# Row 8 of the mirrored matrix dealt into the second sweep, and the third sweep ends with row 7

## The reference, cut to what matters

```
x = layernorm(x + L0(x, adj))      # L0: h = adj @ (adj.T @ e), normalized, + x
T1 = adj @ x                       # L1: a Chebyshev recurrence with K = 4
T2 = 2 * (adj @ T1) - x
T3 = 2 * (adj @ T2) - T1
out = x @ w[0] + T1 @ w[1] + T2 @ w[2] + T3 @ w[3] + bias
x = layernorm(x + out)
```

## Time and profile before

| | |
|---|---|
| median of 3 runs | 1171.82 us (1171.09 to 1174.2) |
| the profiled execution | 1168.52 us, its span 1166.7 us |
| PE busy, share of the span | 1082.1 us, 93% |
| DVE busy | 910.0 us, 78% |
| ACT busy | 330.9 us, 28% |
| DMA | 340.33 MB, 292 GB/s on average |
| mean granted clock of PE | 0.992 |

### The profile page before, as it was taken

The page is one execution under the profiler, slowest core; times in us unless marked ns, Lnnn a source line. Parts: engine busy times, 40 slices in busy tenths (PEclk is TensorE's granted clock), DMA queues, the critical chain, the costliest instruction groups (busy, mean ns, idle before and its releaser), DMA issues.

```text
span 1166.7 us, 13999 instructions
## 1 busy us (share of the span) xinstructions
PE 1082.1 (93%) x5050; PEld 467.6 (40%) x5050; DVE 910.0 (78%) x942; ACT 330.9 (28%) x592; POOL 265.8 (23%) x428
## 2 busy tenths in 40 slices
PE   6898999999999999868889999999899999988897
PEld 5454444444544544412333333443334444422332
DVE  2797788999989989898777767655577877678885
ACT  1555546645655654501111111000110000001111
POOL 0475735644534533610000000000000000001110
PEclk9999999999999999999999999999999999989999
DMA  9999999999999996999999999999599999999991
GB/s 284 273 292 288 285 278 319 301 297 292 270 287 296 273 284 174 224 298 346 278 347 345 327 322 322 296 288 261 163 319 347 337 335 348 338 282 346 343 333 30
DMA packets 366970, 340.33 MB, mean 292 GB/s; under 512 B 17500, under 2 KB 365700, under 8 KB 366932
## 3 DMA queue, kind: packets, MB, share of 16 engines
q1 hardware_dynamic: 257972, 232.24, 70.7%
q10 hardware_dynamic: 106496, 105.00, 31.0%
q0 software_dynamic: 2464, 2.59, 0.9%
HBM read 338.48 MB, written 1.31 MB: 291 GB/s over the span
## 4 chain that ended last, share of the span: by engine, by line
PE 55%; DVE 13%; SPq 12%; ACT 10%; issue 5%; ACTq 1%; POOL 1%; DMA 1%; DVEq 0%; POOLq 0%
PE bank L1267 26%; ACT terms L842 9%; SPq L378 7%; DVE turned L557 6%; PE bank L1335 5%; SPq L367 5%; PE bank L1280 5%; PE bank L1095 2%; PE bank L1135 2%; PE bank L1123 2%; PE bank L1107 2%; DVE shared L577 2%; PE bank L1147 2%; ACTq L321 1%; PE bank L1313 1%
## 5 line engine op out<-in xcount | busy, mean ns | idle before, releaser
L433 POOL COPY raw<-raw 32x512 f32<-32x512 f32 x320 | 195.3, 610 | 241.5 <-DVE raw L594 201.6
L1267 PE MATMUL bank<-turned,terms 128*128 128x512 f32 x528 | 235.5, 597 | 3.2 <-DVE turned L557 2.7
L577 DVE STREAM_TRANSPOSE shared<-shared 32x512 f32<-32x512 f32 x320 | 224.0, 700 | 4.1
L1095 PE MATMUL bank<-shared 128*64 128x256 f32 x1600 | 207.0, 387 | 10.3 <-DMA shared<-in_adj 10.3
L557 DVE STREAM_TRANSPOSE turned<-shared 128x2048 f32<-128x2048 f32 x70 | 160.2, 2301 | 62.4 <-PE bank L1267 34.2
L557 DVE STREAM_TRANSPOSE turned<-raw 128x2048 f32<-128x2048 f32 x70 | 159.7, 2296 | 52.7 <-PE bank L1267 37.4
L842 ACT COPY terms<-terms 32x512 f32<-32x512 f32 x312 | 192.2, 616 | 5.0 <-DVE terms L587 0.9
L326 POOL DMA_DIRECT2D out<-scratch x32 | 17.4, 551 | 597.2 <-DVE scratch L789 597.0
L1267 PEld LDWEIGHTS bank<-turned,terms 128*128 128x128 f32 x528 | 97.9, 190 | 131.1 <-issue 129.1
L1095 PEld LDWEIGHTS bank<-shared 128*64 128x64 f32 x1600 | 112.8, 137 | 92.0 <-issue 33.7
L1335 PE MATMUL bank<-turned,terms 128*64 128x512 f32 x360 | 97.0, 603 | 21.9 <-DVE turned L557 21.9
(11 more groups left out here) (158 smaller groups left out, 1085.7 us busy)
## 6 DMA issues: line engine op xcount, KB each, us to landing
shared<-in_adj SPq DMA_DIRECT2D x100, 1024.0 KB, 10.6
raw<-in_adj SPq DMA_DIRECT2D x100, 512.0 KB, 10.8
raw<-in_adj ACTq DMA_DIRECT2D x100, 512.0 KB, 12.9
shared<-in_adj SPq DMA_DIRECT2D x100, 512.0 KB, 10.5
shared<-in_adj ACTq DMA_DIRECT2D x100, 512.0 KB, 12.3
raw<-in_adj SPq DMA_DIRECT2D x80, 256.0 KB, 7.6
shared<-in_x SPq DMA_DIRECT2D x5, 256.0 KB, 4.7
xq<-in_x POOLq DMA_DIRECT2D x40, 32.0 KB, 6.0
```

The source lines that it names most:

```text
L433: last = nc.gpsimd.tensor_copy(moved[Q32 * c:Q32 * (c + 1), :, :, Q32 * q:Q32 * (q + 1)], beside[Q32 * q:Q32 * (q + 1), :, c, :, :])
L577: last = nc.vector.transpose(low_turned[Q32 * c:Q32 * (c + 1), :, :, Q32 * q:Q32 * (q + 1)], low[Q32 * q:Q32 * (q + 1), :, :, Q32 * c:Q32 ...
L1095: last = nc.tensor.matmul(t_bank[H * odd:H * (odd + 1), 0:PW], e[:, s * SB + b, :], panels[slot][:, s * SB + b, :], start=(k == 0 and b < ...
L1267: last = nc.tensor.matmul(sum_bank[parity][:, :], terms[:, c * GB + i, columns], turned[place][:, i * BANK:(i + 1) * BANK], start=(first a ...
```

## The change

It moves six tiles of T3's row 8, (8,7) to (8,2), from the third sweep into the second, in three pairs behind the three pairs of row 9; DIAG (8,8) and the place of (9,9), (9,8) stay. The second sweep is then n = 0 to 62 and the third n = 63 to 99. The order of what is left in the third sweep is another too: row 7's eight tiles, which stood at its start, stand at its end. Rows 8 and 9 are now open at the same time as two rows of T2, so row 8 is summed in bank 2 and one of the two output banks moves from bank 2 to bank 5. No instruction is added or removed but for waits: the same 100 tiles, 50 loads and 10 output rows are worked in another order.

```diff
-        out_bank = banks[1:3]
+        out_bank = [banks[1], banks[5]]
...
-        ROWS3 = [0, 7, 9, 8, 1, 6, 2, 5, 4, 3]
+        ROWS3 = [0, 9, 6, 8, 1, 5, 2, 4, 3, 7]
...
-        LAST_LOW = [(7, 3), None, (7, 2), (7, 1), (7, 0), (9, 0), (8, 3), (8, 2), (8, 1), (8, 0), (1, 0),
...
+        LAST_LOW = [(6, 2), None, (6, 1), (9, 0), (6, 0), (8, 0), (5, 2), (1, 0), (5, 1), (5, 0), (2, 0), (4, 1), (4, 0),
+                    (3, 1), (3, 0), (7, 3), (7, 2), (7, 1), (7, 0)]
...
                     late += [(DIAG, open_diag, open_diag), (LOW, NG - 1, open_diag + 1), (LOW, NG - 1, open_diag)]
+                    if open_diag < NG - 2:
+                        late += [(LOW, NG - 2, open_diag + 1), (LOW, NG - 2, open_diag)]
                     open_diag = None
```

More of the change, by code:

```diff
@@ L242, in resnorm_chebyshev @@
         ROWS2_ORDER = DOWN[1:]
-        ROWS3 = [0, 7, 9, 8, 1, 6, 2, 5, 4, 3]
-        LOW_BANK = {0: 6, 7: 7, 9: 0, 8: 6, 1: 7, 6: 6, 2: 7, 5: 6, 4: 7, 3: 6}
+        ROWS3 = [0, 9, 6, 8, 1, 5, 2, 4, 3, 7]
+        LOW_BANK = {6: 7, 0: 6, 9: 0, 8: 2, 5: 7, 1: 6, 2: 6, 4: 7, 3: 6, 7: 7}
         UP, DIAG, LOW = range(3)
-        LAST_LOW = [(7, 3), None, (7, 2), (7, 1), (7, 0), (9, 0), (8, 3), (8, 2), (8, 1), (8, 0), (1, 0),
-                    (6, 2), (6, 1), (6, 0), (2, 0), (5, 2), (5, 1), (5, 0), (4, 1), (4, 0), (3, 1), (3, 0)]
+        LAST_LOW = [(6, 2), None, (6, 1), (9, 0), (6, 0), (8, 0), (5, 2), (1, 0), (5, 1), (5, 0), (2, 0), (4, 1), (4, 0),
+                    (3, 1), (3, 0), (7, 3), (7, 2), (7, 1), (7, 0)]
         late = []
```

## The result

| | before | changed |
|---|---|---|
| median of 4 runs each | 1173.01 us (1171.09 to 1174.29) | 1162.9 us (1159.79 to 1163.79) |
| ratio | | 0.991, 95% interval 0.9885 to 0.9935 |
| profiled execution, its span | 1168.52, 1166.7 us | 1163.79, 1162.0 us |

The changed kernel is faster by 0.65 to 1.15%, some 10 us. The two profiled executions differ by 4.7 us only. That is no contradiction, but half of what has to be explained: the profile of before is of a short execution, 4.5 us under its median, and that of the changed kernel lies 0.9 us above its own.

The account below looks back on a forecast made before the run. It took PE and the DMA as near full in the second sweep, DVE with its waits in the third. 14.5 - 1.2 - 17.4 - 4.7 = -8.8 us, taken to the median 1171.82: 1163.0, range 1153 to 1170.

Parts of the forecast that it names:

- Term 1: Second sweep: six more LOW tiles and their loads make it longer, +14.5 us, bounds +10.3 and +18.1.
- Term 2: Change-over from the last UP tile to the first transposition behind row 0's finish: -1.2 us, bounds 0 and -4.5.
- Term 3: DVE's stretch after the change-over: 89.1 us against 106.5, with 6.7 of root waits, -17.4 us, bounds -24.1 and -11.2.
- Rival A: Change-over and third sweep: clock stays up (another -3.3 us), root waits vanish (-2.3 or -6.7), 1153 to 1158; chance 0.20.
- Term 4: The end behind DVE's last transposition: 12.8 us against 17.5, -4.7 us, bounds -4 and -5.
- B: Rows 0, 9, 6, 8 and 1: all three waits whole, change-over as before, gain only -1.4 us, 1170; chance 0.12.
- C: Third sweep: load issues hold ACT ahead of take_p at three rows, +8.9 us, 1181; chance 0.08.
- D: Row 7's last eight tiles: PE's clock falls through short waits, +7 us, 1179; chance 0.03.

Follow-up runs that it names:

- sp_over: The changed kernel with loads 85 to 88 issued by SP in all four quarters, none by ACT: 1176.73 us, ratio 1.0044 to before.
- late_issue: The changed kernel with ACT doing its two output copies behind a row's end before it issues loads: 1156.0 us, ratio 0.9851 to before.
- before_again: The kernel before, unchanged, run once more with a profile: 1178.56 us.
- late_issue5: late_issue with the constant FINISH at 5 instead of 4, a row's finish one tile later: 1171.23 us, ratio 1.0003 to before.
- one_queue: The changed kernel with loads 62 to 69, in the middle of the second sweep, issued by SP alone: 1198.92 us (one run).
- finish5: The changed kernel with the constant FINISH at 5 instead of 4, a row's finish one tile later: 1160.66 us, ratio 0.9908 to before.

## Why the prediction was right, and where it was not

The time (1163.0 said, 1162.9 measured) and the direction hold. Two errors in it cancel nearly, so that the closeness is luck. The sum on the profile was -8.8, and the profiles show -4.7, 4.1 us less. And the difference of 3.3 us from the profile to the median was carried over to the changed kernel, whose median lies 0.9 us under its profile instead.

- *Term 1* (+14.5): +14.1, by the loads as said. The rule "a load lands at the same time whatever tiles it carries" held to 0.5 us.
- *Term 2* (-1.2): -0.9, with the same chain. The queues did stay filled (339 GB/s in the window against 297), and it gave less than 1 us. sp_over and late_issue show the chain's cause: the issue ahead of `take_p`, worth 3.5 us.
- *Term 3* (-17.4): -13.7. The waits were worked out as 4.4, 1.0 and 1.3; they were 4.56, 1.71 and 4.22. The step that failed is the third wait, "row 5's, where PE has caught up in the eight tiles without pairs". The second was sized too short by 0.7 us as well. PE had not caught up: four outputs at 4.3 us had put it behind, a late `take_p` held it 1.47 us more at row 1, and it came level with DVE only at n = 98. In late_issue, without that wait, the same root waits 2.80: so some 1.4 us of the miss are `take_p`'s and the other 1.5 PE's backlog. PE's own work in the stretch, by the prediction's numbers 29 x 1.87 + 8 x 4.3 = 88.6 us, is as large as the 89.1 it gave to DVE, and was not worked out. Rival A's paragraph had it for the outputs, 17 + 22 us of PE against DVE's 36, and the term did not use it. The trace has 89.6 us of PE, and with the 2.9 of waits for `take_p` (rows 1 and 4) and 0.3 for DVE that is the 92.8. late_issue, without the waits for `take_p`, takes 89.3.
- *Term 4* (-4.7): -4.2. PE began the last tile 0.43 us after its transposition was done, so that PE's part was 4.3 us and not 3.9; the 8.9 behind it came as said. The forecast that PE waits in each of the last eight tiles is wrong: it waits once.
- *The clock in the third sweep* stood in no term. The earlier trace rows had 1.00, from one short execution. before_again shows that it can fall there at each pair, and before's runs, 1165.8 to 1178.6 in all, hold both kinds. By the medians (-10.1) and the profiles (-4.7), about 5 us of the result come from before's longer executions. It is probably no accident: before's order makes PE wait 2.4 us at each pair, the changed one has no such wait for DVE, and the mean clock of the runs is 0.989 and 0.993. The prediction got these 5 us without naming them, by carrying over 3.3 us that it did not explain. That the spread is the clock's alone is not shown: what lies ahead of the late list varied by some 4 us too.
- *Rival A* (the clock stays up, -3.3 more): it did not in the changed kernel; late_issue is that case. *B*: one pair waited whole in it as in before, the last nearly. *C*: its mechanism is real at the change-over; behind it the issues are short (0.9 to 1.4 us for two), as said, and what rows 1 and 4 lose, 1.47 us each, is another wait, that of the issue for its slot. In late_issue5 C's mechanism decides the time. The prediction called itself wrong if PE waits for ACT's copies at several rows: it did at rows 0, 1 and 4, 6.1 us in all, but only row 0's was by a held issue, and the time held. *D*: the clock stays at 1.00 in row 7's tiles, with no waits there that could test it.

## What to carry to other kernels

An engine that issues DMAs into a queue that may be full shouldn't stand before a copy that another engine waits for: put the copy first, and count the held issues anew after each further edit. Add up the work of every engine for a stretch, not only of the one that limits it now; here the second was 0.5 us away. And take the profile's own time against the spread of the runs before a difference of a few us is read from it.

## What was not expected of the hardware

- SP's queue alone moved 216 GB/s (one_queue, 940 to 950 us), its packets at 112.6% of the 16 engines' time; with ACT's beside it the two moved 347 at 110.3%.
- Two DMA instructions of a load's quarters held ACT for 3.0 to 6.6 us around the change-over in most traces (6.39, 6.21, 6.35 and 6.57 the longest of four of them), and 0.9 to 1.4 us in the changed kernel's stretch. That a full queue makes the difference is inferred, no view shows the queue's filling.
- PE's granted clock, between its two levels 2.4 and 1.2 GHz, fell behind a wait of 3.21 us (the LOW tile behind it took 3.68 us, not 1.9) and behind one of 4.41 (3.03 us). It stayed up in finish5, where PE waited 2.5 us at the same place. The wait alone doesn't decide it: behind waits of 2.40 and 2.41 us a LOW tile took 3.37 us in one execution of before and 1.94 in another.
